# Context rounding moved from ScalarE to GpSimd from the second batch on, with the five engine orders drawn up anew

## The chip, the cores and the metric

The kernel runs on one core of one Trainium2 chip. The metric is the device time of one execution in microseconds (us), the median of several runs. Engines are named as in the profile: PE (TensorE matmuls), PEld (its weight loads), DVE (VectorE), ACT (ScalarE), POOL (GpSimd), SP (SyncE, which issues every DMA here).

## The reference

A gated cross-attention block with a feed-forward network on 16 batches of 224 queries (512 wide) that look at 750 context rows (384 wide):

```python
q = (layernorm(x) @ W_q); k = (context @ W_k); v = (context @ W_v)      # 8 heads of 64
attn = softmax(where(mask, q k^T / 8, -max))
x = x + tanh(g_xattn[0]) * ((attn @ v) @ W_o + b_o)
h = gelu(bitlinear(layernorm(x), w1, b1))
x = x + tanh(g_ffn[0]) * bitlinear(h, w2, b2)
```

`bitlinear` scales each row to 127 levels and the weights to -1, 0 and 1 around the mean of their absolute values, and then multiplies.

## The kernel before

Float32 operands of the attention are split into two float16 tiles, an upper half (the value rounded) and a lower half (the value less its upper half), and every product is three float16 matmuls. The context of a batch is three chunks of 128 x 750 (`KC` = 3). Each chunk is loaded by SP into one of two slots of `ctx_f` (kind LC in the orders); ACT rounds it into `ctx[:, 0, n, :]` (L1199, kind CX), POOL subtracts that from the float32 value into `ctx[:, 1, n, :]` (L1310, also kind CX). `ctx` has one buffer, so the rounding of a batch waits until PE has done all 8 key products (K) and 6 value products (V) of the batch before (`k_proj`, `v_proj`), and the first K or V of a batch waits for `ctx_lo` of all three chunks. The third chunk of a batch takes the slot of the first, so its load waits for the first chunk's subtraction.

PE's other kinds: Q (query products), S (scores), PV (weights times values), O (output projection), F1 and F2 (the two feed-forward products), WM (a product that sums the feed-forward weights' means). The softmax of a batch is 14 units: DVE adds the mask and finds the row extreme (L978, M), ACT takes the exponential (L1157, E) and divides (L1162, N), POOL rounds (L1301, H) and subtracts (L1306, L), and SP turns both halves by a transposing DMA (L740, T) for PV. A slot of `p16` (4) is free again when that DMA has landed.

The feed-forward weights come in 16 float32 pieces: ACT sums absolute values (L1147, WA) into `wabs` and writes a throwaway result into `rough`, which lies over `xc`; after WM, POOL scales each piece (L1290, WB) and DVE clips it (L965, WQ). The first F1 waits for all 16 (`w_quant`). `b1` is loaded (BD) when ten pieces are done.

Nothing is scheduled at run time. Each engine goes through a written list of kind:number:batch (`SP_SEQ`, `PE_SEQ`, `ACT_SEQ`, `DVE_SEQ`, `POOL_SEQ`), and semaphores hold an engine until its operands are there. PE results go through a ring of four PSUM banks, `ps_g0` to `ps_g3`, taken in turn in the order of `PE_SEQ`.

Of the kernel before, what the change touches and what calls it, by code (L numbers as in the profile page):

```python
# [17 lines left out]
HT = TQ // 2  # L18
# [4 lines left out]
NT = 6  # L23
# [4 lines left out]
H = 8  # L28
# [44 lines left out]
def in_order(text):  # L73
# [10 lines left out]
    LC:2:3 XT:1:3 T:1:2 T:0:2 T:3:2 XQ:0:1 T:2:2 LC:1:4 T:4:2 LC:0:4 T:5:2 F2:1:0 LM:0:3 XQ:1:1 T:6:2 LR:1:2 T:7:2
    T:8:2 HT:0:1 T:9:2 LR:0:2 T:11:2 T:12:2 T:10:2 T:13:2 HT:1:1 LC:2:4 T:0:3 LX:0:5 F2:0:1 T:1:3 XT:1:4 XT:0:4
    XQ:0:2 F2:1:1 T:2:3 T:3:3 LR:0:3 T:4:3 T:6:3 LM:0:4 T:5:3 XQ:1:2 T:7:3 T:8:3 T:9:3 LC:0:5 HT:0:2 LR:1:3 T:11:3
    LC:1:5 T:12:3 T:10:3 T:13:3 LC:2:5 LX:0:6 XT:0:5 LM:0:5 XT:1:5 F2:0:2 HT:1:2 T:0:4 XQ:0:3 T:2:4 T:1:4 LR:1:4
    T:3:4 T:4:4 XQ:1:3 F2:1:2 T:5:4 T:6:4 T:7:4 HT:0:3 LC:1:6 T:8:4 LC:0:6 T:9:4 T:10:4 T:11:4 LX:0:7 T:13:4 T:12:4
    XT:0:6 F2:0:3 XT:1:6 HT:1:3 T:0:5 T:1:5 T:2:5 LC:2:6 T:3:5 LM:0:6 T:4:5 T:5:5 LR:0:5 T:6:5 LC:1:7 T:7:5 XQ:1:4
    F2:1:3 T:8:5 LR:1:5 T:9:5 LC:0:7 T:11:5 T:12:5 T:10:5 T:13:5 LM:0:7 LX:0:8 LC:2:7 LR:0:6 XT:0:7 XT:1:7 T:0:6  # L90
    HT:1:4 T:1:6 T:2:6 XQ:0:5 T:3:6 T:4:6 F2:1:4 T:5:6 T:6:6 T:7:6 LC:1:8 LC:0:8 LR:1:6 T:9:6 T:8:6 XQ:1:5 T:10:6
    LM:0:8 HT:0:5 T:11:6 T:12:6 T:13:6 LC:2:8 LX:0:9 XT:1:8 XT:0:8 T:0:7 HT:1:5 T:1:7 T:3:7 T:2:7 XQ:0:6 T:4:7
    F2:1:5 T:5:7 F2:0:5 LR:1:7 LC:0:9 T:7:7 T:6:7 T:9:7 LR:0:7 LC:1:9 XQ:1:6 T:8:7 HT:0:6 T:11:7 T:10:7 T:13:7
# [10 lines left out]
    T:2:13 LM:0:14 T:3:13 T:4:13 F2:1:11 XQ:1:12 T:5:13 LR:1:13 LC:0:15 T:6:13 T:7:13 T:9:13 T:8:13 LM:0:15 T:11:13
    T:10:13 T:12:13 T:13:13 XT:0:15 HT:1:12 LC:2:15 T:0:14 T:1:14 F2:1:12 T:2:14 T:3:14 XQ:0:13 T:5:14 T:4:14
    XT:1:15 T:6:14 LR:0:14 T:7:14 XQ:1:13 HT:0:13 T:8:14 T:9:14 LR:1:14 T:11:14 T:10:14 T:13:14 T:12:14 F2:0:13
    LR:0:15 T:0:15 T:1:15 T:2:15 HT:1:13 T:3:15 XQ:0:14 T:4:15 F2:1:13 T:5:15 T:6:15 T:7:15 T:8:15 LR:1:15 T:9:15
    T:10:15 HT:0:14 T:11:15 T:12:15 T:13:15 F2:1:14 F2:0:14 F2:0:15 F2:1:15
# [351 lines left out]
def build(nc, x_d, ctx_d, mask_d, gx_d, gf_d, wq_d, wk_d, wv_d, wo_d, bo_d, w1_d, b1_d, w2_d, b2_d, out_d):  # L460
    with ExitStack() as stack:
# [937 lines left out]
```

## Time and profile before

| What | Value |
|---|---|
| Median of 3 runs | 1027.44 us (1027.41 to 1028.69) |
| Profiled execution | 1028.62 us, its span 1026.7 us |
| Busy share of the span | PE 95%, ACT 84%, DVE 78%, POOL 76% |
| Costliest line | `ps_g` products of L776, 38% of the chain that ended last |

The span is the part of the execution that the trace covers; the other 1.9 us lie around it. Busy time of matmuls is modelled, so a share of 95% on PE tells that it was seldom without work, not that it ran at its peak. An engine that is idle costs time only where PE, or the end, waits for it.

### The profile page before, as it was taken

How to read it: one execution, taken by the hardware profiler on the slowest of the kernel's cores; microseconds unless marked ns; L12 is line 12 of the kernel's file. 1: busy time of each engine (PE TensorE's matmuls, PEld its weight loads, DVE VectorE, ACT ScalarE, POOL GpSimd, SP SyncE). 2: the span in 40 equal slices, each digit the busy share in tenths (PEclk: the TensorE clock that was granted, in tenths of full speed). 3: DMA queues.
4: the chain of work that ended last, by engine and by line, in shares of the span. 5: the costliest groups of instructions: out<-in, count | busy, mean ns of one | idle time of the engine just before them, and what ended most of it. 6: DMA issues, size and time to landing. Idle time of an engine off the chain costs nothing.

```text
span 1026.7 us, 25406 instructions
## 1 busy us (share of the span) xinstructions
PE 977.3 (95%) x9216; PEld 562.0 (55%) x9216; DVE 800.2 (78%) x1870; ACT 860.0 (84%) x1386; POOL 779.3 (76%) x739
## 2 busy tenths in 40 slices
PE   3979898999999999999999999999999999999887
PEld 2536555565555656555555555555565556556443
DVE  6669788868998677977769778877868776876766
ACT  4879777988879879897888889798897977889866
POOL 3599998787678787877678696877687688867861
PEclk9989999999999999999999999999999999999989
DMA  6999979997879988978879798897888888778961
GB/s 229 239 212 244 206 159 157 177 163 135 189 142 173 187 168 157 169 130 172 155 153 172 157 187 162 137 174 142 169 163 182 166 167 153 138 133 162 168 100 41
DMA packets 472331, 169.10 MB, mean 165 GB/s; under 512 B 450320, under 2 KB 452368, under 8 KB 471824
## 3 DMA queue, kind: packets, MB, share of 16 engines
q1 hardware_dynamic: 472208, 167.48, 83.5%
q8 instruction: 75, 1.23, 0.5%
q14 instruction: 48, 0.39, 0.1%
HBM read 48.28 MB, written 7.34 MB: 54 GB/s over the span
## 4 chain that ended last, share of the span: by engine, by line
PE 68%; DVE 9%; POOL 6%; ACT 6%; DMA 5%; issue 4%; SPq 1%; DVEq 0%; POOLq 0%; ACTq 0%
PE ps_g L776 38%; PE ps_g L826 9%; PE ps_s L809 8%; PE ps_g L864 8%; PE ps_g L901 5%; POOL p L1306 3%; DMA pt<-p 2%; DVE xa L1021 2%; DVE prob L978 1%; POOL ctx L1310 1%; POOL p L1301 1%; ACT prob L1157 1%; ACT prob L1162 1%; DVE xc L1047 1%; ACT h_sb L1255 1%
## 5 line engine op out<-in xcount | busy, mean ns | idle before, releaser
L1306 POOL TENSOR_TENSOR p<-prob,p 128x750 f16<-128x750 f32 x224 | 357.8, 1608 | 4.8
L1301 POOL CAST p<-prob 128x750 f16<-128x750 f32 x224 | 186.0, 835 | 125.7 <-ACT prob L1162 100.1
L978 DVE CUSTOM_DVE_ANT_0 prob<-ps_s,mbias 128x750 f32<-128x750 f32 x224 | 205.8, 933 | 51.3 <-PE ps_s L809 35.2
L1157 ACT ACTIVATE prob<-prob,rmin 128x750 f32<-128x750 f32 x224 | 204.5, 914 | 26.2 <-DVE rmin L978 25.3
L1162 ACT ACTIVATE prob<-prob,rrec 128x750 f32<-128x750 f32 x224 | 198.7, 914 | 29.5 <-DVE rrec L923 29.3
L776 PE MATMUL ps_g<-ctx,wk 128*128 128x375 f16 x1152 | 201.1, 327 | 18.1 <-POOL ctx L1310 17.4
L776 PE MATMUL ps_g<-wv,ctx 128*128 128x512 f16 (+1 forms) x864 | 198.3, 379 | 1.2 <-DVE k_sb L1000 0.6
L776 PEld LDWEIGHTS ps_g<-ctx,wk 128*128 128x128 f16 x1152 | 110.9, 99 | 100.9 <-issue 29.6
L776 PEld LDWEIGHTS ps_g<-wv,ctx 128*128 128x128 f16 (+1 forms) x864 | 86.4, 103 | 97.3 <-issue 6.5
L809 PE MATMUL ps_s<-k_sb,q_sb 64*32 64x375 f16 (+2 forms) x2688 | 129.4, 325 | 7.7 <-DVE k_sb L1000 4.4
L826 PE MATMUL ps_g<-pt,v_sb 128*64 128x224 f16 (+2 forms) x2448 | 121.6, 256 | 4.5 <-DMA pt<-p 4.1
L826 PEld LDWEIGHTS ps_g<-pt,v_sb 128*64 128x64 f16 x2448 | 109.3, 111 | 23.0 <-issue 16.6
L864 PE MATMUL ps_g<-w,xqt 128*128 128x512 fp8e4 x432 | 103.6, 384 | 3.6 <-ACT xqt L1218 2.0
L901 PE MATMUL ps_g<-w,hqt 128*128 128x512 fp8e4 x432 | 97.7, 379 | 3.1 <-DMA hqt<-hq 2.4
L809 PEld LDWEIGHTS ps_s<-k_sb,q_sb 64*32 64x32 f16 (+2 forms) x2688 | 62.4, 95 | 65.5 <-issue 40.2
L1310 POOL TENSOR_TENSOR ctx<-ctx_f,ctx 128x750 f16<-128x750 f32 x47 | 74.1, 1585 | 17.8 <-ACT ctx L1199 17.3
L1075 DVE SCALAR_TENSOR_TENSOR h_sb<-ps_g,sm,b 128x512 f32<-128x512 f32 x108 | 76.8, 744 | 11.3 <-PE ps_g L864 10.7
L994 DVE SCALAR_TENSOR_TENSOR v_sb<-ps_g,v_sb 128x512 f16<-128x512 f32 x96 | 64.9, 685 | 24.3 <-ACT v_sb L1187 23.9
L776 PE MATMUL ps_g<-xt,wq 128*128 128x224 f16 x768 | 82.1, 259 | 0.7 <-DVE wv L931 0.4
L1000 DVE SCALAR_TENSOR_TENSOR k_sb<-ps_g,k_sb 128x375 f16<-128x375 f32 x128 | 67.8, 542 | 18.2 <-ACT k_sb L1174 18.0
L776 PEld LDWEIGHTS ps_g<-xt,wq 128*128 128x128 f16 x768 | 71.9, 98 | 12.9 <-issue 5.3
L776 PE MATMUL ps_g<-wo,attn 128*128 128x512 f16 x336 | 76.7, 380 | 1.3 <-DVE attn L988 1.3
(129 smaller groups left out, 1328.6 us busy)
## 6 DMA issues: line engine op xcount, KB each, us to landing
ctx_f<-in_ctx SPq DMA_DIRECT2D x47, 375.0 KB, 4.0
xa<-in_x SPq DMA_DIRECT2D x16, 448.0 KB, 4.7
xr<-in_x SPq DMA_DIRECT2D x28, 256.0 KB, 3.4
out<-xr SPq DMA_DIRECT2D x28, 256.0 KB, 2.9
pt<-p SPq DMA_TRANSPOSE x254, 4.1
h_sb<-in_w SPq DMA_DIRECT2D x4, 512.0 KB, 5.7
w<-in_w SPq DMA_DIRECT2D x3, 512.0 KB, 6.1
xr<-in_w SPq DMA_DIRECT2D x3, 512.0 KB, 5.0
```

What stands on the lines that cost most here:

```text
L776: mm = nc.tensor.matmul(out, lhs, rhs, start=(m == 0), stop=(m == len(steps) - 1))
L809: mm = nc.tensor.matmul(ps_s[at:at + width, e, c, 0:CH], q_sb[rows, j, qa, q:q + width], k_sb[rows, j, ka, c * CH:(c + 1) * CH], start=(m ...
L826: mm = nc.tensor.matmul(g[e * DH:(e + 1) * DH, 0:size], v_sb[:, p, t, va, (2 * j + e) * DH:(2 * j + e + 1) * DH], pt[:, e, pa * NT + t, pl ...
L864: mm = nc.tensor.matmul(g[:, :], xqt_t[:, k, :], w1v[:, k, f * 512:(f + 1) * 512], start=(k == 0), stop=(k == KD - 1))
L901: mm = nc.tensor.matmul(g[:, :], hqt_t[:, k, :], w2v[:, k, :], start=(k == 0), stop=(k == KF - 1))
L978: nc.vector.tensor_tensor_reduce(prob[:, (b * NU + n) % PROBS, :].rearrange("p (c k) -> p c k", c=2), ps_s[:, n % 2, :, 0:CH], mbias[:, :] ...
L1075: nc.vector.scalar_tensor_tensor(out=h_t[:, f * 512:(f + 1) * 512], in0=g[:, :], scalar=sm2[:, t % 2, 4:5], in1=b1[:, f * 512:(f + 1) * 51 ...
L1157: nc.scalar.activation(prob[:, (b * NU + n) % PROBS, :], prob[:, (b * NU + n) % PROBS, :], ACT.Exp, bias=rmin[:, n:n + 1], scale=-1.0, acc ...
L1162: nc.scalar.activation(held, held, ACT.Copy, scale=rrec[:, n:n + 1]).then_inc(normed, 1)
L1301: nc.gpsimd.tensor_copy(p16[:, u % HILO, 0, 0:J], prob[:, u % PROBS, :]).then_inc(hi_pool, 1)
L1306: nc.gpsimd.tensor_tensor(p16[:, u % HILO, 1, 0:J], prob[:, u % PROBS, :], p16[:, u % HILO, 0, 0:J], ALU.subtract).then_inc(lo_pool, 1)
L1310: nc.gpsimd.tensor_tensor(ctx[:, 1, n, :], ctx_place(b * KC + n), ctx[:, 0, n, :], ALU.subtract)\
```

## The change

ACT keeps the rounding of the context for the first batch only. For batches 1 to 15 POOL does it, just ahead of its own subtraction of the same chunk, with the waits that ACT had. That is 45 instructions. All five lists are drawn up anew. DVE gets two waits at tile 0: the feed-forward's `xc` is written only when all of ACT's sums of absolute values are done (they write into the same place), and the scale is taken only after the second WM.

```diff
@@ lists: 5 of 5 redrawn; the first line of PE_SEQ's second row stands for them @@
-    V:4:0 V:5:0 K:7:0 S:4:0 Q:3:0 WM:0:0 S:5:0 K:0:1 K:1:1 PV:0:0 V:0:1 S:6:0 V:1:1 Q:0:1 K:2:1 K:3:1 Q:1:1 Q:2:1
...
@@ DVE, L2 @@
                     need_tile(dve, "xq", t - 1)
+                    if t == 0:
+                        dve.wait_ge(w_abs, 2 * NW)
                     nc.vector.tensor_scalar(xc[:, :], xr_t, mv2[:, c, 0:1], None, ALU.subtract)\
...
@@ DVE, L3 @@
                     need_tile(dve, "x2_amp", t)
+                    if t == 0:
+                        need(dve, "w_mean", 0, 1)
...
@@ ACT @@
-                elif kind == "CX":
+                elif kind == "CX" and b == 0:
                     need_ctx(act, b * KC + n)
-                    need(act, "k_proj", b - 1, 2 * NP - 1)
-                    need(act, "v_proj", b - 1, NT - 1)
                     nc.scalar.activation(ctx[:, 0, n, :], ctx_place(b * KC + n), ACT.Copy)\
                         .then_inc(s["ctx_hi"], 1)
...
@@ POOL @@
                 elif kind == "CX":
+                    if b > 0:
+                        need_ctx(pool, b * KC + n)
+                        need(pool, "k_proj", b - 1, 2 * NP - 1)
+                        need(pool, "v_proj", b - 1, NT - 1)
+                        nc.gpsimd.tensor_copy(ctx[:, 0, n, :], ctx_place(b * KC + n)).then_inc(s["ctx_hi"], 1)
                     need(pool, "ctx_hi", b, n)
                     nc.gpsimd.tensor_tensor(ctx[:, 1, n, :], ctx_place(b * KC + n), ctx[:, 0, n, :],
```

POOL where the context of batch 1 is made, before (`winv` marks the scaling of weight pieces, `p16` the halves of the softmax):

```order
27 L1301 CAST p16<-prob 128x750
28 L1310 TENSOR_TENSOR ctx<-ctx_f,ctx 128x750
29 L1306 TENSOR_TENSOR p16<-prob,p16 128x750
30 L1290 TENSOR_SCALAR w12<-w12,winv 128x1024
31 L1310 TENSOR_TENSOR ctx<-ctx_f,ctx 128x750
32 L1290 TENSOR_SCALAR w12<-w12,winv 128x1024
33 L1310 TENSOR_TENSOR ctx<-ctx_f,ctx 128x750
```

and after:

```order
30 L1311 CAST ctx<-ctx_f 128x750
31 L1313 TENSOR_TENSOR ctx<-ctx_f,ctx 128x750
32 L1311 CAST ctx<-ctx_f 128x750
33 L1313 TENSOR_TENSOR ctx<-ctx_f,ctx 128x750
34 L1304 TENSOR_TENSOR p16<-prob,p16 128x750
35 L1311 CAST ctx<-ctx_f 128x750
36 L1313 TENSOR_TENSOR ctx<-ctx_f,ctx 128x750
37 L1288 TENSOR_SCALAR w12<-w12,winv 128x1024 x2
```

The two weight pieces that stood between the chunks stand behind them now, and three casts are new.

PE from the last value products of batch 0 to the first key product of batch 1, before:

```order
19 L776 MATMUL ps_g2<-wv,ctx 128x512 x9
20 L776 MATMUL ps_g3<-wv,ctx 110x512 x9
21 L776 MATMUL ps_g0<-ctx,wk 128x375 x9
22 L809 MATMUL ps_s<-k_sb,q_sb 128x375 x12
23 L776 MATMUL ps_g1<-xt,wq 128x224 x12
24 L783 MATMUL ps_g2<-wsum,xqt 128x1
25 L809 MATMUL ps_s<-k_sb,q_sb 32x375 x48
26 L776 MATMUL ps_g3<-ctx,wk 128x375 x9
```

and after:

```order
19 L772 MATMUL ps_g3<-ctx,wk 128x375 x9
20 L772 MATMUL ps_g0<-wv,ctx 110x512 x9
21 L805 MATMUL ps_s<-k_sb,q_sb 64x375 x24
22 L805 MATMUL ps_s<-k_sb,q_sb 128x375 x12
23 L772 MATMUL ps_g1<-xt,wq 128x224 x12
24 L779 MATMUL ps_g2<-wsum,xqt 128x1
25 L805 MATMUL ps_s<-k_sb,q_sb 32x375 x48
26 L772 MATMUL ps_g3<-ctx,wk 128x375 x9
```

One scores unit (64x375, 24 matmuls) moved behind the last value product; the same set of products stands ahead of the first key product of batch 1.

POOL up to the last two weight pieces (those in `h_sb`), before:

```order
73 L1290 TENSOR_SCALAR hq<-hq,winv 128x1024
74 L1306 TENSOR_TENSOR p16<-prob,p16 128x750
75 L1301 CAST p16<-prob 128x750
76 L1290 TENSOR_SCALAR hqt<-hqt,winv 128x1024
77 L1306 TENSOR_TENSOR p16<-prob,p16 128x750
78 L1290 TENSOR_SCALAR xr<-xr,winv 128x1024
79 L1290 TENSOR_SCALAR h_sb<-h_sb,winv 128x1024 x2
```

and after:

```order
79 L1288 TENSOR_SCALAR w12<-w12,winv 128x1024
80 L1288 TENSOR_SCALAR hq<-hq,winv 128x1024
81 L1288 TENSOR_SCALAR hqt<-hqt,winv 128x1024
82 L1299 CAST p16<-prob 128x750
83 L1288 TENSOR_SCALAR xr<-xr,winv 128x1024
84 L1304 TENSOR_TENSOR p16<-prob,p16 128x750
85 L1288 TENSOR_SCALAR h_sb<-h_sb,winv 128x1024 x2
```

The pieces moved a little among the softmax units; counted from the start of the list, everything that stood ahead of the last piece still does, with six context casts (batches 1 and 2) besides.

## Rows read from the trace of the kernel before

**Rows 1.** The page's first part: busy us, share of the span, instructions.

```profile
PE 977.3 (95%) x9216; PEld 562.0 (55%) x9216; DVE 800.2 (78%) x1870; ACT 860.0 (84%) x1386; POOL 779.3 (76%) x739
```

**Rows 2.** Busy time by stretch: start:end, length, engines, granted PE clock, DMA share, GB/s.

```profile
0.00:50.00 50.00, 33.80 (x270) 18.73 (x270) 33.31 (x57) 33.58 (x56) 24.06 (x30) 1.00 0.84 235
50.00:100.00 50.00, 41.89 (x390) 24.37 (x388) 40.41 (x86) 42.17 (x80) 48.18 (x37) 0.90 1.01 219
100.00:150.00 50.00, 46.17 (x500) 28.85 (x496) 40.00 (x93) 37.70 (x68) 46.60 (x42) 1.00 0.93 199
150.00:200.00 50.00, 47.29 (x415) 26.42 (x414) 42.02 (x105) 43.76 (x72) 39.73 (x39) 1.00 0.89 163
...
950.00:1000.00 50.00, 42.44 (x462) 22.55 (x460) 35.72 (x89) 38.35 (x54) 38.65 (x41) 0.90 0.77 136
1000.00:1026.70 26.70, 20.32 (x119) 9.45 (x116) 18.55 (x37) 16.32 (x26) 3.11 (x6) 0.98 0.10 40
```

**Rows 3.** The same view for the middle, 200 to 950 us.

```profile
200.00:950.00 750.00, 745.39 (x7077) 431.63 (x7076) 590.18 (x1410) 648.14 (x1035) 579.00 (x550) 1.00 0.85 161
```

**Rows 4.** PE in order of time, 31 to 66 us: start, us, [idle before <-releaser].

```profile
31.25 3.05 PE L776 MATMUL ps_g<-ctx,wk 128*128 128x375 f16 x18
...
47.64 1.60 PE L776 MATMUL ps_g<-ctx,wk 128*128 128x375 f16 x9
...
53.74 0.38 PE L783 MATMUL ps_g<-wsum,xqt 128*128 128x1 f32 x2 [1.93 <-DVE wsum L958]
58.51 2.08 PE L809 MATMUL ps_s<-k_sb,q_sb 64*32 64x375 f16 x48 [4.39 <-DVE k_sb L1000]
61.74 5.34 PE L776 MATMUL ps_g<-ctx,wk 128*128 128x375 f16 x18 [1.15 <-POOL ctx L1310]
```

**Rows 5.** POOL in order of time, the same place.

```profile
54.99 2.12 POOL L1290 TENSOR_SCALAR w<-w,winv 128x1024 f32<-128x1024 f32 x1 [1.27 <-DVE winv L950]
...
58.57 1.55 POOL L1290 TENSOR_SCALAR w<-w,winv 128x1024 f32<-128x1024 f32 x1
```

**Rows 6.** Groups by line and shape: count, busy us, mean ns, idle before.

```profile
L1301 POOL CAST p<-prob 128x750 f16<-128x750 f32 x224 | 186.0, 835 | 125.7 <-ACT prob L1162 100.1 <-DMA pt<-p 24.5
L1310 POOL TENSOR_TENSOR ctx<-ctx_f,ctx 128x750 f16<-128x750 f32 x47 | 74.1, 1585 | 17.8 <-ACT ctx L1199 17.3
L1199 ACT ACTIVATE ctx<-ctx_f 128x750 f16<-128x750 f32 x47 | 38.2, 823 | 8.1 <-DMA ctx_f<-in_ctx 6.9 <-issue 1.0
```

**Rows 7.** The page's DMA part: issues, KB each, us to landing.

```profile
ctx_f<-in_ctx SPq DMA_DIRECT2D x47, 375.0 KB, 4.0
```

**Rows 8.** POOL, DVE and PE around the last weight pieces, and POOL's wait before them.

```profile
121.45 0.81 POOL L1301 CAST p<-prob 128x750 f16<-128x750 f32 x1 [1.80 <-DMA pt<-p]
...
132.96 2.64 POOL L1290 TENSOR_SCALAR h_sb<-h_sb,winv 128x1024 f32<-128x1024 f32 x2
...
134.99 2.36 DVE L965 TENSOR_SCALAR w<-h_sb 128x1024 fp8e4<-128x1024 f32 x2
...
137.83 3.63 PE L864 MATMUL ps_g<-w,xqt 128*128 128x512 fp8e4 x16
```

**Rows 9.** PE's waits, 130 to 200 us: us in total, times, longest.

```profile
PE ps_g L901 <- DMA hqt<-hq: 1.6, 1, 1.6
PE ps_g L826 <- DMA pt<-p: 0.9, 1, 0.9
```

**Rows 10.** PE in order of time: an output projection, and a second feed-forward product.

```profile
105.58 2.75 PE L776 MATMUL ps_g<-wo,attn 128*128 128x512 f16 x12
...
957.58 3.61 PE L901 MATMUL ps_g<-w,hqt 128*128 128x512 fp8e4 x16
```

**Rows 11.** L1021 alone: shortest, median, longest ns.

```profile
L1021 DVE TENSOR_SCALAR xa<-xa,mv x32: 474/1022/5655, 9.9 to 853.7; 112x512 f32<-112x512 f32 x32
```

**Rows 12.** PE's waits, 950 us to the end, the longest two.

```profile
PE ps_s L809 <- DVE rmin L978: 2.2, 1, 2.2
PE ps_g L864 <- ACT xqt L1218: 2.0, 2, 1.3
```

More of the change, by code:

```diff
@@ L84 @@
[L84 to L93, printed above, removed]
@@ L104 @@
[L104 to L108, printed above, removed]
+    PD:0:0 LX:0:0 LC:0:0 LC:1:0 LC:2:0 PD:1:0 PD:2:0 XT:0:0 XT:1:0 WL:0:0 LM:0:0 WL:1:0 LC:0:1 WL:2:0 LX:0:1 LM:0:1
@@ new lines @@
+    WL:7:0 WL:5:0 WL:6:0 WL:3:0 T:0:0 WL:4:0 T:1:0 LC:1:1 BD:0:0 LC:2:1 PD:3:0 T:2:0 T:4:0 LC:0:2 T:3:0 XT:0:1
+    XT:1:1 T:5:0 LX:0:2 T:6:0 WL:8:0 T:7:0 WL:9:0 LR:1:0 T:9:0 T:8:0 WL:11:0 WL:13:0 WL:10:0 T:10:0 WL:12:0 T:11:0
+    T:13:0 WL:15:0 T:12:0 LC:1:2 WL:14:0 LC:2:2 T:0:1 LM:0:2 T:1:1 XT:0:2 XT:1:2 T:2:1 LC:0:3 T:3:1 LX:0:3 T:5:1
+    T:4:1 T:6:1 T:7:1 XQ:1:0 BD:1:0 LR:1:1 LR:0:1 T:8:1 T:9:1 T:10:1 LM:0:3 T:11:1 LR:0:2 T:12:1 LC:1:3 T:13:1
+    HT:1:0 LX:0:4 XT:0:3 XT:1:3 LC:2:3 T:0:2 T:1:2 XQ:0:1 F2:1:0 T:2:2 T:3:2 T:5:2 T:4:2 T:7:2 XQ:1:1 T:6:2 T:8:2
@@ new lines @@
+    LR:1:8 T:5:8 T:7:8 XQ:1:7 T:9:8 T:8:8 F2:1:6 LC:1:10 HT:0:7 T:11:8 T:10:8 T:13:8 T:12:8 LX:0:11 LM:0:10 T:0:9
+    HT:1:7 LC:2:10 XT:0:10 XT:1:10 T:2:9 T:1:9 T:3:9 F2:0:7 T:4:9 LR:0:9 LR:1:9 XQ:1:8 T:5:9 T:6:9 T:7:9 T:8:9
+    LC:0:11 LM:0:11 T:10:9 T:9:9 LX:0:12 T:11:9 T:13:9 T:12:9 XT:1:11 LC:1:11 XT:0:11 F2:1:7 HT:1:8 T:0:10 LR:0:10
+    LC:2:11 T:1:10 XQ:0:9 T:2:10 T:3:10 LC:0:12 T:4:10 XQ:1:9 T:5:10 F2:1:8 LC:1:12 T:6:10 LX:0:13 T:7:10 T:9:10
+    T:8:10 HT:0:9 T:10:10 T:11:10 T:12:10 T:13:10 LR:1:10 T:0:11 LC:2:12 F2:0:9 T:1:11 XT:1:12 LR:0:11 HT:1:9
@@ new lines @@
+    Q:1:11 N:4:10 L4:0:9 N:5:10 E:8:10 N:6:10 XH:0:12 XH:1:12 N:7:10 E:9:10 N:8:10 L4:1:9 K:0:11 K:1:11 GE:0:9
+    K:2:11 V:0:11 E:10:10 E:11:10 N:9:10 PL:0:10 V:1:11 GS:0:9 V:2:11 N:10:10 E:12:10 V:3:11 N:11:10 K:3:11 G3:0:9
+    K:4:11 E:13:10 E:0:11 N:12:10 PL:1:10 E:1:11 N:13:10 K:5:11 N:0:11 GE:1:9 V:4:11 K:6:11 K:7:11 GS:1:9 E:2:11
+    V:5:11 PL:2:10 N:1:11 PL:3:10 E:3:11 E:4:11 N:2:11 E:5:11 Q:2:11 N:3:11 G3:1:9 Q:3:11 N:4:11 N:5:11 L4:0:10
+    K:0:12 V:0:12 E:6:11 E:7:11 E:8:11 N:6:11 N:7:11 E:9:11 K:1:12 GE:0:10 XH:0:13 V:1:12 E:10:11 V:2:12 Q:0:12
@@ new lines @@
+    N:11:12 E:0:13 N:12:12 N:13:12 K:4:13 E:1:13 K:5:13 PL:1:12 GE:1:11 N:0:13 XH:1:14 K:6:13 N:1:13 GS:1:11 V:4:13
+    E:2:13 K:7:13 E:3:13 G3:1:11 E:4:13 N:2:13 PL:2:12 PL:3:12 V:5:13 E:5:13 Q:3:13 N:3:13 N:4:13 N:5:13 E:6:13
+    E:7:13 V:0:14 K:0:14 N:6:13 L4:1:12 E:8:13 N:7:13 E:9:13 V:1:14 V:2:14 N:8:13 Q:0:14 N:9:13 K:1:14 PL:0:13
+    E:10:13 E:11:13 E:12:13 N:10:13 E:13:13 K:2:14 XH:0:15 K:3:14 N:11:13 XH:1:15 K:4:14 N:12:13 E:0:14 N:13:13
+    E:1:14 V:3:14 Q:1:14 N:0:14 GE:1:12 N:1:14 K:5:14 PL:1:13 E:2:14 E:3:14 Q:2:14 Q:3:14 V:4:14 V:5:14 GS:1:12
@@ new lines @@
+    GM:1:7 VL:4:9 VL:5:9 XH:1:10 QL:2:9 G2:1:7 M:4:9 F2:0:7 PA:2:8 PA:3:8 M:5:9 M:6:9 M:7:9 KL:6:9 N1:0:11 QL:3:9
+    KL:7:9 R:2:9 XN:0:11 R:3:9 O:1:8 L2:1:8 M:8:9 F2:1:7 QL:0:10 M:9:9 QL:1:10 KL:0:10 L3:1:8 XH:0:11 KL:1:10
+    KL:2:10 M:10:9 R:4:9 M:11:9 PA:0:9 F1:4:8 VL:0:10 VL:1:10 R:5:9 M:12:9 M:13:9 F1:5:8 KL:3:10 F1:6:8 R:6:9
+    XH:1:11 F1:7:8 KL:4:10 M:0:10 M:1:10 PA:1:9 M:2:10 VL:2:10 VL:3:10 GM:1:8 R:0:10 VL:4:10 M:3:10 VL:5:10 G2:1:8
+    KL:5:10 KL:6:10 R:1:10 N1:0:12 M:4:10 KL:7:10 QL:2:10 M:5:10 PA:2:9 PA:3:9 XN:0:12 M:6:10 QL:3:10 M:7:10 O:0:9
```

448 lines of the change are left out of this document (217 added, 231 removed).

## The prediction

> **What bounds the kernel now.** I read the page's first part, then the busy time by stretch, then in each stretch where PE idles the order of time and the waits. PE is busy 977.3 of 1026.7 us, ACT 860.0, DVE 800.2, POOL 779.3 [rows 1]. The stretches tell where PE's missing 49.4 us lie: 16.2 in the first 50 us, 8.1, 3.8 and 2.7 in the next three, 7.6 and 6.4 at the end [rows 2], and only 750 - 745.4 = 4.6 us in all the 750 us between [rows 3]. So PE is the bound from 200 to 950 us, and a change that gives PE no less work can win nothing much there; it can lose. What can be won lies between 50 and 200 us (14.6 us of idle time, and in part a lower clock) and after 950 us (14.0 us). The first 16 us are unchanged, since batch 0's context stays with ACT.
>
> Between 50 and 100 us POOL is busy 48.2 of 50 us, from 100 to 150 us 46.6 of 50 [rows 2]. That is the stretch in which POOL scales the feed-forward weights beside the softmax, and it is where the change gives it more.
>
> **What is moved.** ACT loses 45 roundings of 823 ns, 37.0 us. POOL gains 45 casts. The trace has the same cast on POOL, same shape and types, at 835 ns [rows 6]: 45 x 0.835 = 37.6 us, 2.5 us a batch. POOL's share goes from 76% to (779.3 + 37.6) / 1026.7 = 80%, ACT's from 84% to 80%. Neither is the bound by its total. From a chunk's arrival to its lower half the time is the same (0.82 + 1.59 against 0.84 + 1.59), but where ACT rounded the second chunk beside POOL's first subtraction, POOL now does both: the three chunks take 3 x 2.42 = 7.3 us of POOL, against 0.82 + 3 x 1.59 = 5.6 us, 1.7 us more a batch. DVE's two new waits cost nothing: in its own list the sum over all 16 absolute sums and the second WM already stand ahead of them.
>
> **Place 1, the context of batch 1.** Before, PE ends the last key product of batch 0 at 47.64 + 1.60 = 49.2, and starts batch 1 at 61.74, having waited 1.93, 4.39 and 1.15 us between [rows 4]. POOL held it: it idled 1.27 us for the weights' mean, then two weight pieces (2.12 and 1.55 us) stood ahead of the second and third chunk [rows 5]. After, these pieces stand behind. I take the end of batch 0's products at 49.6 (0.4 later, since its last value product now waits for a bank that DVE frees later). POOL then needs 7.3 us and one softmax subtraction of 1.6: 58.5. The third chunk's load starts when the first chunk is done (52.0), takes 0.3 to issue and 4.0 to land [rows 7], so the chunk is done at 56.3 + 2.4 = 58.7. Batch 1 starts at about 58.9, 2.8 us earlier. From both sides: 4 us if the products end at 48.4, 1 us if the load takes as long as 5.8.
>
> **Place 2, the first feed-forward product.** That lead has to survive until F1, which waits for all 16 weight pieces. Before, POOL ended its last piece at 132.96 + 2.64 = 135.6, DVE the clip at 137.3, and PE started F1 at 137.83 [rows 8]; the wait was just covered. POOL is the queue to count here. At about 61.4 it has done the same work in both kernels (the two pieces follow at 58.7, 2.7 us), with three of the new casts already behind it; before, that was at 61.6. From there to the last piece its list holds the same instructions and three more casts, 2.5 us. It had one idle time of 1.80 us there [rows 8] that may be filled. So the last piece ends at 135.6 - 0.2 + 2.5 less 0 to 1.8 = 136.1 to 137.9, I take 137.0. DVE's clip adds 1.7, as before: F1 at 138.7, 0.9 us later than before (0 to 1.8). PE's work ahead of F1 is the same set in both, so here **the whole 2.8 us is given back** and PE waits. This step decides the sum.
>
> **Place 3, 140 to 200 us.** Two waits of PE stand there, 1.6 us for the turned hidden layer and 0.9 us for turned softmax weights [rows 9]. The first hangs on ACT, which has six roundings less behind it, 6 x 0.82 = 4.9 us; it should go. The second hangs on POOL, which is not faster; it stays. I take -1.3, between -2.5 (both go) and +1.5 (POOL late by the third batch's 2.5 us).
>
> **Place 4, the middle.** Thirteen batches from the fourth on. In the new list PE has between 11.4 and 24.5 us of other products after a batch's last key or value product and before the next batch's first, counted with their durations in the trace (an output projection 2.7 and a second feed-forward product 3.5 us [rows 10], some 1.1 us for a scores unit or a query product); POOL has the chunks and what stands between them, 7.3 us and one to four others. The tightest are batch 10 (11.4 us on PE against 7.3 + 1.6 + 0.8 + 0.9 = 10.6 on POOL), batch 15 (12.5 against 10.9) and batch 14 (12.9 against 11.2). Their margins, 0.8 to 1.7 us, hold if POOL comes to them on time. Before, the margins at the same places were 2.3, 1.3 and 4.9. I take +0.7 for the middle, from -1 (ACT's relief takes some of the 4.6 us) to +5.
>
> In the same stretch DVE's L1021 takes 474 ns at best, 1022 in the middle and 5655 at worst [rows 11], in places where POOL works without a pause. The Trainium skill, page "SBUF — State Buffer", section "Who interferes with whom", gives a rule that speaks against the change: a DVE instruction in a two-port mode and a GpSimd instruction take one port pair in turn, and the second fully waits. The trace agrees. By it, DVE's excess at L1021 (32 x (1.022 - 0.474), about 18 us by the median) would grow with POOL's busy time, by 4.8%, some 0.9 us on an engine with 22% idle: the sum would be the same or up to 1 us more.
>
> **Place 5, the end.** The last seven scores and the last tiles keep their order in the main. The two longest waits are 2.2 and 2.0 us [rows 12]. The last scores' row extremes now come ahead of a layer norm on DVE, which takes most of the first; the copy of the turned tile on ACT (the second wait) then stands behind two more normalisations, 1.8 us. I take -0.3, between -2 and +2.
>
> **The sum.** +0.9 (places 1 and 2 together) - 1.3 + 0.7 - 0.3 = 0.0 against the profiled 1028.62 us (span 1026.7). That execution lies at the upper end of the three runs, so against the median of 1027.44 the same sum gives 1027.4 us.
>
> **Rivals.** First, **the lead survives** (faster): POOL reaches its last weight piece early, because it has fewer idle or stretched instructions between 60 and 140 us than I count, and PE's lead of 2.8 us stays, with the waits of place 3. 1027.4 - 0.9 - 2.8 - 1.2 = 1022.5. For it: one place already has POOL idle 1.8 us; against it: POOL has 48.2 of 50 us filled [rows 2]. Chance 0.27. Second, **POOL becomes the gate of each batch's context** (slower): the new 1.7 us per batch falls on PE wherever the margin is used up, which needs POOL to be more than 0.8 to 1.7 us late at its first chunk in the tight batches. Three tight batches only: 3 x 1.7 = +5; half of the thirteen: 6.5 x 1.7 = +11. I take +5, 1032.4. For it: POOL was idle 125.7 us before its casts, waiting for ACT and DMA [rows 6], so it does not run ahead of its work; against it: PE had no wait for the context anywhere in the middle. Chance 0.20. Third, **the clock**: after the idle time at 50 to 60 us 18 key matmuls took 5.34 us at a lower granted clock against 3.05 us at 31 us [rows 4], and the stretch 50 to 100 us has a mean of 0.90 [rows 2]. If the shorter gap keeps the clock up, 2.3 us (and 1 us at the scores ahead) come back, but go into the wait at F1 like the rest; if PE's new wait before F1 (about 3.7 us) brings the clock down, the same 3 us are lost, and stay lost: 1030.5. Chance 0.10. **The change does not do what it says** only if the cast on POOL were dearer than L1301's, at the 1.6 us of a subtraction: 45 x 0.77 = 35 us more of POOL, and the second rival comes true; 0.03, counted there.
>
> **How the numbers follow.** Forecast, within its own range 1025 to 1030: 0.43. The rivals have 0.27 (faster), 0.20 (slower) and 0.10 (slower). A measurement tells apart some 0.2%, 2.05 us. Faster by that: most of the first rival and the lower edge of the forecast, 0.30. Slower: the second, most of the third and the upper edge, 0.31. Within: 0.39. The range takes in the first rival with both waits gone and something won at the end (1021.5), and the second up to four tight batches (1034).
>
> **What would show it.** In the profile of the changed kernel: the first key product of batch 1 at 58 to 60 us; a wait of PE at the first F1 (L860) of 2 to 4 us for DVE's clip, and F1 at 138 to 139.5; L1311 at 0.83 to 0.85 us x45; no longer a wait of 1.6 us for the turned hidden layer; PE busy over 744 us from 200 to 950, with waits for POOL's context absent or under 1 us. It would be wrong if F1 starts before 137, or if PE waits for L1313 in more than three batches, or if the end, from the last key product on, is longer or shorter by over 2 us.

## The result, and the profile of the changed kernel

| | kernel before | changed kernel |
|---|---|---|
| median | 1027.43 us (1027.35 to 1028.69) | 1035.97 us (1035.74 to 1036.46) |
| profiled execution, span | 1026.7 us | 1034.5 us |
| PE idle in the span | 49.4 us | 57.7 us |

The change makes the kernel slower: 1.0072 of before, 95% interval 1.0058 to 1.0087; the medians differ by 8.5 us, the profiled spans by 7.8. The forecast was 1027.4 us, no change, within 1021.5 to 1034, and the time is outside that range. One execution of a later kernel, the one with M:9:12 moved, took 4039 us and is left out of its ratio.

The first part of the page of the changed kernel, against [rows 1]:

```profile
PE 976.8 (94%) x9216; PEld 562.0 (54%) x9216; DVE 801.3 (77%) x1870; ACT 829.0 (80%) x1341; POOL 816.2 (79%) x784
```

PE has the same work. POOL has 36.9 us more. ACT has 31.0 us less: its rounding alone fell from 38.2 to 1.7 us. PE's busy time by stretch (start:end, length, PE, PEld, DVE, ACT, POOL, granted clock, DMA share, GB/s), first of the changed kernel:

```profile
0.00:200.00 200.00, 167.79 (x1552) 97.36 (x1553) 157.81 (x335) 150.50 (x262) 166.17 (x152) 0.99 0.88 200
200.00:780.00 580.00, 575.84 (x5426) 333.94 (x5425) 455.39 (x1099) 481.80 (x773) 474.94 (x458) 1.00 0.87 164
780.00:800.00 20.00, 16.29 (x118) 7.86 (x116) 16.10 (x29) 7.91 (x14) 12.24 (x15) 0.83 0.67 127
800.00:950.00 150.00, 148.08 (x1406) 86.08 (x1405) 112.38 (x267) 125.41 (x201) 114.29 (x107) 1.00 0.82 148
```

and of the kernel before:

```profile
780.00:800.00 20.00, 19.64 (x179) 10.32 (x177) 17.32 (x36) 17.28 (x25) 14.38 (x14) 1.00 0.71 151
```

One stretch of 20 us stands out: PE does 118 matmuls there and not 179, and the granted clock falls to 0.83. To see whether the loss is there, I compared the start of each PE item at which both order lists have issued the same set of items. The changed kernel is 3.2 us ahead at the first key product of batch 1 (61.7 against 58.5), 1.8 behind at the first F1 (137.8, 139.6), even at the first F2 (162.3, 162.4), and from then to O:1:11 (773.7, 774.7) never more than 1.2 us away from it, and 1 us behind at that point. At the next shared point, V:5:13, it is 7.4 us behind (824.8, 832.2), and it ends 7.7 behind. So **about 6.4 us are lost between 775 and 832 us**, and one event near 784 us accounts for them. DVE in order of time there (start, us, then in brackets the idle time before and its releaser):

```profile
783.29 0.68 DVE L1038 BATCH_NORM_STATS2 st<-xr 128x6 f32<-128x512 f32 x1
784.00 0.18 DVE L1040 BATCH_NORM_AGGREGATE mv<-st 128x2 f32<-128x6 f32 x1
784.22 5.56 DVE L1045 TENSOR_SCALAR xc<-xr,mv 128x512 f32<-128x512 f32 x1
789.81 0.69 DVE L1048 TENSOR_REDUCE sm<-xc 128x1 f32<-128x512 f32 x1
790.42 0.93 DVE L974 CUSTOM_DVE_ANT_0 prob<-ps_s,mbias 128x750 f32<-128x750 f32 x1
```

L1045 (L1047 before) takes the mean off the residual row tile in its layer norm, L2:1:11. Its 28 instances take 485 ns at best and 830 in the middle; before, 486, 658, and 1939 at most. This one took 5.56 us. POOL in the same stretch:

```profile
782.46 3.08 POOL L1304 TENSOR_TENSOR p<-prob,p 128x750 f16<-128x750 f32 x2
785.50 2.48 POOL L1350 TENSOR_TENSOR xr<-xr,gb 128x512 f32<-128x512 f32 x2
787.94 1.56 POOL L1299 CAST p<-prob 128x750 f16<-128x750 f32 x2
789.86 1.26 POOL L1350 TENSOR_TENSOR xr<-xr,gb 128x512 f32<-128x512 f32 x1 [0.36 <-DVE xc L1045]
```

POOL's instructions follow each other without a gap until 789.50. There POOL itself stops, since its next entry, L3:1:11, needs this very xc, and 0.28 us later DVE is done. None of these POOL instructions is one of the new casts: two softmax subtractions, two additions of gb2 (the last part of L3:1:10 and L3:0:11) and two softmax casts. PE behind it:

```profile
786.19 1.60 PE L772 MATMUL ps_g<-ctx,wk 128*128 128x375 f16 x9
791.50 2.08 PE L805 MATMUL ps_s<-k_sb,q_sb 64*32 64x375 f16 x48 [3.71 <-DVE rmin L974]
793.51 5.50 PE L860 MATMUL ps_g<-w,xqt 128*128 128x512 fp8e4 x16
```

The scores S:5:12 wait 3.71 us for the minimum that stands behind xc in DVE's list; then 48 score matmuls take 2.08 us (1.15 elsewhere, as in the experiments below) and 16 of F1 5.50 us where 3.63 are usual [rows 8]. From 780 to 790 us the granted clock is 1.00, from 790 to 800 us 0.66: in part of that stretch PE had the lower of its two levels (1.2 for 2.4 GHz), after it had stood idle. The wait and the slower matmuls are 3.7 + 0.9 + 1.9 = 6.5 us, as much as the jump.

### The profile page after: what moved, and what is told of

Read it like the earlier page. It is cut to its first block, busy times and chain, and to the rows that moved or that the text cites. A ratio compares the mean times of both kernels' runs of the same rounds, so it can differ in the third digit from the quotient of the medians.

```text
span 1034.5 us, 25408 instructions
## 1 busy us (share of the span) xinstructions
PE 976.8 (94%) x9216; PEld 562.0 (54%) x9216; DVE 801.3 (77%) x1870; ACT 829.0 (80%) x1341; POOL 816.2 (79%) x784
## 3 DMA queue, kind: packets, MB, share of 16 engines
q8 instruction: 75, 1.23, 0.5%
## 4 chain that ended last, share of the span: by engine, by line
PE 60%; POOL 13%; DVE 10%; issue 7%; ACT 5%; DMA 4%; SPq 1%; POOLq 0%; DVEq 0%; ACTq 0%
PE ps_g L772 33%; PE ps_g L822 7%; PE ps_s L805 7%; PE ps_g L860 6%; PE ps_g L897 5%; POOL p L1304 5%; POOL p L1299 3%; DVE prob L974 2%; DVE xc L1045 2%; DMA pt<-p 2%; POOL ctx L1313 2%; ACT prob L1157 1%; DVE st L1038 1%; DVE xa L1017 1%; SPq L736 1%
## 5 line engine op out<-in xcount | busy, mean ns | idle before, releaser
L1299 POOL CAST p<-prob 128x750 f16<-128x750 f32 x224 | 183.6, 829 | 107.9 <-ACT prob L1162 86.7
L990 DVE SCALAR_TENSOR_TENSOR v_sb<-ps_g,v_sb 128x512 f16<-128x512 f32 x96 | 64.6, 683 | 18.0 <-ACT v_sb L1187 17.8
```

The costliest lines, as they stand in the source:

```text
L1299: nc.gpsimd.tensor_copy(p16[:, u % HILO, 0, 0:J], prob[:, u % PROBS, :]).then_inc(hi_pool, 1)
```

## Experiments

**Theory:** the casts and their order cost nothing together; the loss is DVE's subtraction held off by an unbroken run of POOL work, which the redrawn order happens to make. **Rivals:** the 37 us more of POOL work are the loss; or the redrawn order as a whole is. Times on different chips differ by some 2 us for the same kernel, so I compare ratios to the kernel before run beside each. The expectations give ranges in us; where a time of its own chip would put a run elsewhere in them than its ratio does (the ratio times 1027.4 us), I go by the ratio and say so.

**The move alone.** All five lists are those of the kernel before; POOL's and ACT's code is changed, and DVE has its two new waits at tile 0. In part:

```
-                elif kind == "CX":           (ACT)
+                elif kind == "CX" and b == 0:
+                    if b > 0:                (POOL)
+                        nc.gpsimd.tensor_copy(ctx[:, 0, n, :], ctx_place(b * KC + n)).then_inc(s["ctx_hi"], 1)
```

> The move of the rounding alone: the program of the changed kernel with the five order lists of the kernel before, so that GpSimd makes the 45 casts (0.83 us each) at the places of its own subtractions and ScalarE skips its entries. Theory (the changed kernel loses its 8 us in one event near 784 us, where the subtraction xc<-xr,mv on VectorE took 5.56 us while GpSimd ran without a pause, and that event belongs to the redrawn order): the casts cost next to nothing, 1026 to 1030 us, no xc<-xr,mv over 2.5 us. Rival (the 37 us of added work on GpSimd are the loss): 1032 to 1037 us, with TensorE waiting for the context or for the turned weights in many batches. Second rival (the casts bring the gain of the first 200 us, and the order gives it back): 1022 to 1025 us.

Measured: 1.0133 of before (1.0109 to 1.0157), some 14 us slower, above even what the rival gave; the theory fails here, as it had the casts at next to nothing. The loss is not in one place: against the kernel before it is 4.6 us by the first F2, 6.1 by V:0:4, 8.5 by S:6:8, 10.1 by V:0:13 and 14.1 by V:0:15. One xc took 3.01 us. In PE's waits (total, times, longest), POOL's context has

```profile
PE ps_g L776 <- POOL ctx L1317: 23.5, 7, 16.0
```

where the kernel before has 17.4 us in 3 times; the 16 us at the start are in both. That is 6.1 of the 14 us; the rest is not assigned. What the cast costs apart from held subtractions, the last experiment tells.

**The order alone.** The lists of the changed kernel, rounding by ACT in every batch. ACT's list of the changed kernel has no such entries, so I put them behind the drain or exponential that they followed before, and never ahead of K:7 and V:5 of the last batch; batch 12:

```
-    V:5:11 PL:2:10 N:1:11 PL:3:10 E:3:11 E:4:11 N:2:11 E:5:11 Q:2:11 N:3:11
+    V:5:11 CX:0:12 PL:2:10 N:1:11 PL:3:10 E:3:11 E:4:11 N:2:11 E:5:11 Q:2:11 CX:1:12 CX:2:12 N:3:11
```

> The redrawn order alone: the five order lists of the changed kernel, but the context's upper halves rounded by ScalarE in every batch, its 45 entries put back into ScalarE's list behind the same drain or exponential as in the kernel before; GpSimd keeps only the subtraction. Theory: the run of GpSimd work near 780 to 789.5 us holds no cast, so the event stays, with one xc<-xr,mv of 4 to 6 us and a total of 1033 to 1038 us. Rival (the added work on GpSimd): no cast, no loss, 1026 to 1029 us. Were ScalarE's 33 us at these places now late, waits of TensorE for probabilities would show in many batches, and neither would be borne out.

Measured: 1.0643 (1.0616 to 1.0669), 66 us slower, far outside both. POOL now waits for ACT's rounding in each batch (groups by line; before, this line had 17.8 us of idle time [rows 6]):

```profile
L1312 POOL TENSOR_TENSOR ctx<-ctx_f,ctx 128x750 f16<-128x750 f32 x47 | 74.3, 1585 | 77.6 <-ACT ctx L1201 77.6
```

PE's delay grows at the batch starts, from K:0:1 on. The places of ACT's entries are mine, so this is not the price of the order, only a sign that it can't do with ACT's rounding put in so. But it shows one thing cleanly. With no cast on POOL the event is there again, with the same POOL instructions around it. DVE and then POOL:

```profile
831.20 5.55 DVE L1047 TENSOR_SCALAR xc<-xr,mv 128x512 f32<-128x512 f32 x1
```

```profile
829.43 3.08 POOL L1308 TENSOR_TENSOR p<-prob,p 128x750 f16<-128x750 f32 x2
832.47 2.48 POOL L1349 TENSOR_TENSOR xr<-xr,gb 128x512 f32<-128x512 f32 x2
834.91 1.56 POOL L1303 CAST p<-prob 128x750 f16<-128x750 f32 x2
```

PE waits 4.20 us behind it. The event belongs to the order, not to the casts.

**The run cut short.** Two entries of POOL's list:

```
-    H:4:12 H:5:12 L:4:12 L:5:12 L3:1:10 L3:0:11 H:6:12 H:7:12 L3:1:11 L2:1:11
+    H:4:12 H:5:12 L:4:12 L:5:12 H:6:12 H:7:12 L3:1:11 L2:1:11
```

with L3:1:10 behind L:13:11 and L3:0:11 behind G2:0:11.

> The changed kernel with two entries of GpSimd's list moved, nothing else: the additions of gb2 to the tiles L3:1:10 and L3:0:11, which stand next to each other inside the long run, go to where the kernel before has them (behind L:13:11, and behind G2:0:11). Theory: the run of GpSimd near 784 us is broken, xc<-xr,mv there takes under 2.5 us, TensorE's wait of 3.71 us in front of the scores and the slow matmuls behind it go: 1028 to 1030.5 us. Rival (the loss is spread over the order or the casts and the event only coincides with it): 1034 to 1037 us.

Measured: 1.0044 (1.0029 to 1.0059), 1031.9 us by the ratio, between the two, and the longest xc is 3.12 us and not under 2.5. The expectation was wrong in one point: the run does not end there, since the two casts close up behind the subtractions. It is shorter by 2.48 us, and xc by 2.44. DVE's line alone (ns: shortest, median, longest), PE's wait, and POOL:

```profile
L1045 DVE TENSOR_SCALAR xc<-xr,mv x28: 486/686/3120, 114.2 to 1004.7; 128x512 f32<-128x512 f32 x28
```

```profile
790.65 1.15 PE L805 MATMUL ps_s<-k_sb,q_sb 64*32 64x375 f16 x48 [1.27 <-DVE rmin L974]
```

```profile
784.05 3.09 POOL L1304 TENSOR_TENSOR p<-prob,p 128x750 f16<-128x750 f32 x2
787.08 1.57 POOL L1299 CAST p<-prob 128x750 f16<-128x750 f32 x2
789.01 1.26 POOL L1350 TENSOR_TENSOR xr<-xr,gb 128x512 f32<-128x512 f32 x1 [0.36 <-DVE xc L1045]
```

**The run made longer.** One more sum of constant tiles on POOL behind L3:0:11:

```
+                    nc.gpsimd.tensor_tensor(extra[:, :], gbo[:, :], gb2[:, :], ALU.add)
```

> The changed kernel with one more GpSimd instruction in the long run: a sum of two constant 128x512 tiles into a scratch tile that nothing reads, behind L3:0:11; its output is not used. If VectorE's subtraction is held until GpSimd's run ends, it takes 5.56 plus 1.0 to 1.3 us, 6.5 to 6.9 us, and the kernel 1036.5 to 1039 us. Rival (VectorE gets its turn after a fixed time, or after so many instructions): it stays at 5.6 us or below, and the total at 1035 to 1036.5 us.

The added instruction takes 1.27 us, and xc 6.79, 1.23 more than 5.56. At this place DVE gets no turn after a time or a number of instructions: it waits for POOL's pause. In every trace that has the event (the changed kernel, the order alone, the run cut short, the run made longer, and the one below with M:9:12 moved) xc ends 0.28 us after POOL's pause begins.

```profile
783.54 6.79 DVE L1046 TENSOR_SCALAR xc<-xr,mv 128x512 f32<-128x512 f32 x1
```

```profile
784.82 2.50 POOL L1354 TENSOR_TENSOR xr<-xr,gb 128x512 f32<-128x512 f32 x2
787.26 1.27 POOL L1296 TENSOR_TENSOR extra<-gbo,gb 128x512 f16<-128x512 f32 x1
788.47 1.58 POOL L1303 CAST p<-prob 128x750 f16<-128x750 f32 x2
```

```profile
792.05 2.08 PE L806 MATMUL ps_s<-k_sb,q_sb 64*32 64x375 f16 x48 [4.95 <-DVE rmin L975]
794.07 4.23 PE L861 MATMUL ps_g<-w,xqt 128*128 128x512 fp8e4 x16
```

The total, 1.0076 (1.005 to 1.0102), is the same as that of the changed kernel within the intervals; by the ratio it is 1035.2 us, so the hold came out as the theory had it and the total as the rival had it. PE waited 4.95 us in place of 3.71, but F1 took 4.23 us in place of 5.50 (granted clock 0.83 from 790 to 800 us, 0.66 in the changed kernel). The longer hold cost nothing more, because a shorter part of the work fell to the low clock.

**Another form of the instruction.** The same subtraction, in the form that also sums its output (into an unused column):

```
-                    nc.vector.tensor_scalar(xc[:, :], xr_t, mv2[:, c, 0:1], None, ALU.subtract)\
+                    nc.vector.tensor_scalar(xc[:, :], xr_t, mv2[:, c, 0:1], 0.0, ALU.subtract, ALU.add,
+                                            accum_out=sm2[:, c, 7:8])\
```

 Rival (something else stopped VectorE there, or the order as a whole is slow): an instance of over 4 us stays, or goes without a gain, 1034 to 1037 us.

Measured: 0.9973 of before (0.9958 to 0.9987), 1024.7 us by the ratio and below the theory's range, which is about what the one event alone would give; the changed kernel is now faster than the kernel before. All 28 instances take the same time, though POOL's run stands where it stood (781.22 here, 785.50 there; start, us):

```profile
L1045 DVE TENSOR_SCALAR_CACHE_REDUCE xc<-xr,mv x28: 745/746/747, 112.1 to 996.9; 128x512 f32<-128x512 f32 x28
```

```profile
780.45 0.75 DVE L1045 TENSOR_SCALAR_CACHE_REDUCE xc<-xr,mv 128x512 f32<-128x512 f32 x1
```

```profile
778.18 3.08 POOL L1304 TENSOR_TENSOR p<-prob,p 128x750 f16<-128x750 f32 x2
781.22 2.50 POOL L1350 TENSOR_TENSOR xr<-xr,gb 128x512 f32<-128x512 f32 x2
783.67 1.56 POOL L1299 CAST p<-prob 128x750 f16<-128x750 f32 x2
```

```profile
783.67 1.15 PE L805 MATMUL ps_s<-k_sb,q_sb 64*32 64x375 f16 x48
784.76 3.63 PE L860 MATMUL ps_g<-w,xqt 128*128 128x512 fp8e4 x16
```

The plain form and POOL's run must both be there for the hold. The Trainium skill has this in "SBUF — State Buffer", section "Who interferes with whom": copies and scalar operations of DVE can take a two-port mode and then share a port pair with GpSimd, "not the form that also writes out its accumulator". The trace agrees, 745 to 747 ns in all 28 instances, one of them inside the same POOL run.

The time from S:4:12 to V:5:13, the same PE work in all kernels with the changed PE list, measures the event: 54.8 us in the changed kernel, 50.1 with the run cut, 54.8 with it longer, 48.2 with the summing form (and 48.2 in both runs below that have the summing form for xa too). **The event costs 6.6 us.**

**Who stands behind the held instruction.** One entry of DVE's list:

```
-    L3:0:11 R:3:12 QL:0:13 VL:0:13 L2:1:11 M:9:12 KL:0:13
+    L3:0:11 R:3:12 QL:0:13 VL:0:13 M:9:12 L2:1:11 KL:0:13
```

> The changed kernel with one entry of VectorE's list moved: the mask and minimum M:9:12, for which TensorE's scores wait, stands ahead of L2:1:11, whose subtraction is held. The hold stays (4.3 to 5.6 us, since GpSimd's run is as long as before), but no scores wait behind it. Theory (the price is what queues behind the held instruction on VectorE): TensorE's wait of 3.71 us in front of the scores goes, another of 0 to 2 us for k_sb or for the drains of the first F1 takes its place, total 1030 to 1033 us. Rival (the held tile's own chain sets the loss): 1034.5 to 1036.5 us.

Measured: 1.0029 (1.0014 to 1.0045), by the ratio 1030.4 us, in the theory's range. xc takes 3.74 us, less than the 4.3 to 5.6 expected, since it starts later in the same run, the scores wait for nothing, and a wait of 1.49 us comes up in the middle of F1:

```profile
787.50 3.74 DVE L1044 TENSOR_SCALAR xc<-xr,mv 128x512 f32<-128x512 f32 x1
```

```profile
789.16 1.15 PE L804 MATMUL ps_s<-k_sb,q_sb 64*32 64x375 f16 x48
790.24 1.04 PE L859 MATMUL ps_g<-w,xqt 128*128 128x512 fp8e4 x4
792.77 2.76 PE L859 MATMUL ps_g<-w,xqt 128*128 128x512 fp8e4 x12 [1.49 <-DVE q_sb L1000]
```

The stretch S:4:12 to V:5:13 takes 49.9 us, so this gives back 4.9 of the 6.6 us, some of it through the shorter hold.

**What the change is worth without the hold.** The summing form in the kernel before, first for xc alone, then in either kernel for xc and for xa<-xa,mv (L1021, the same operation on the input rows, [rows 11]).

> The kernel before in its own order, with the same edit as in the one-port run of the changed kernel: xc<-xr,mv in the form that also sums its output (0.745 us in every instance there, where it took 0.658 us in the median and 1.94 at most before). What the held-off subtraction costs the kernel before. Theory: it never was held long there, so little changes, 1026 to 1028.5 us, and the changed kernel with the same edit (0.9973 of before) stays 1 to 3 us faster than this one: that difference is the gain of the change itself with the contention taken out. Rival (the one-port form is a gain of its own in any order): this kernel falls by as much as the changed one against its own former time by more than the one event, to 1023 to 1025 us, and the change itself is worth nothing.

> The changed kernel with both subtractions of VectorE that the two-port form serves (xc<-xr,mv of 28 tiles and xa<-xa,mv of 32 half tiles) in the form that also sums its output. xa<-xa,mv is still held there up to 5.65 us at 10 us, before the first context is ready, and 2.0 to 3.1 us for a pair in five batches. Theory: each pair falls to 1.5 to 1.7 us; at 10 us the held one goes, GpSimd's rs comes earlier or not at all, since TensorE waits for GpSimd's context there and not for xa; total 1023 to 1026.5 us. Rival (all of it was in the one event): the same as the run with xc alone, 1026.4 us, within 0.7 us; or slower by up to 1 us through 32 longer instructions.

> The kernel before, in its own order, with xc<-xr,mv and xa<-xa,mv both in the form that also sums its output: the counterpart of the changed kernel with both (0.9938 of before, interval 0.992 to 0.9957). It says what the change is worth when GpSimd can hold neither subtraction. Theory (with the event gone the change is worth next to nothing, as 0.9973 against 0.9971 with xc alone said): 0.993 to 0.997 of before, 1022.5 to 1025.5 us where before is at 1028, within 2 us of the changed kernel. Rival (the change gains 2 to 4 us that the contention had hidden): 0.9965 to 0.999, over 2.5 us behind the changed kernel of the same form.

> The changed kernel with both subtractions in the summing form, the same program as before, now beside its counterpart on one chip. Theory: 0.992 to 0.996 of before, and within 2 us of the counterpart. Rival: over 2.5 us ahead of it.

Ratios to the kernel before, with their intervals (the two of the middle row come from two chips):

| form of the two subtractions | order and code before | changed kernel |
|---|---|---|
| both plain | 1 | 1.0072 (1.0058 to 1.0087) |
| xc summing | 0.9971 (0.9953 to 0.9989) | 0.9973 (0.9958 to 0.9987) |
| both summing | 0.9933 (0.9911 to 0.9955) | 0.9943 (0.9924 to 0.9962), and 0.9938 (0.992 to 0.9957) on another chip |

Read down, the summing form gains 7 us in the kernel before and 13 in the changed one, though every instance is longer than the plain form at its best (746 against 486 ns; xa 740 against 474). With xc alone the kernel before gains 3 us, where the theory had "little changes": its rival was right, a gain in any order. With both forms its gain is in many small pieces: 1.8 us by the first F2, 4.4 by K:1:6, 7.2 by F1:5:11. The 5.65 us at the start [rows 11] are gone too, and win nothing: at K:0:1 the two are level within 0.5 us. The changed kernel with both gained more than expected, 1021.1 us by the ratio for 1023 to 1026.5. Read across, the change is worth nothing once nothing is held: the differences are within their intervals. The 1 to 3 us that I expected the changed kernel to keep over the other with the same form are not there. All four summing kernels are faster than both kernels of the case; the kernel before with both forms had the lowest median, 1022.21 us beside 1029.6 for the kernel before.

**The move alone, without the hold.**

> The move of the rounding alone (order lists of the kernel before, casts on GpSimd), now with both subtractions in the summing form. With them in the two-port form it took 1.0133 of before, 13 us more. Theory (that loss is the casts standing in an order that was not drawn for them: TensorE waits 6 us more for the context and more through the drains behind it, in many batches, with a single held subtraction of 3.0 us): most stays, 1034 to 1039 us, 6 to 10 us above before. Rival (it too is VectorE held by a busier GpSimd): it goes, 1025 to 1030 us.

Measured: 1.0045 (1.0031 to 1.0058), a median of 1034.3 us. That is 4.7 us above before and not 6 to 10, and 1032.0 us by the ratio, between the two ranges: neither had counted what the summing form gains in any order. So the run to compare with is the kernel before with the same forms (1022.21 us on the same chip), and against it this one is 12 us slower, where the plain forms gave 14. So most of what the casts cost in the old order, 12 us, has nothing to do with held subtractions, and the redrawn order wins these 12 us back, since the changed kernel with both forms is level with the kernel before.

## Why the prediction was wrong, point by point

- **The amount of work moved** was right: L1311 takes 853 ns on average x45 (808 in the middle, 1272 at most), POOL 816.2 us (816.9 forecast).
- **Place 1** was right in its time, K:0:1 at 58.50, forecast 58.9, and 3.2 us earlier than before for 2.8, but in part by luck. Batch 0's products ended at 47.7 us and not at 49.6, so POOL's third chunk was done at 57.3 and not at 58.7; what then stood ahead of K:0:1 was PE's own scores, up to 58.5. PE in order of time, against [rows 4]:

```profile
55.15 0.38 PE L779 MATMUL ps_g<-wsum,xqt 128*128 128x1 f32 x2 [2.00 <-DVE wsum L954]
56.54 2.03 PE L805 MATMUL ps_s<-k_sb,q_sb 64*32 64x375 f16 x48 [1.01 <-DVE q_sb L1001]
58.50 2.36 PE L772 MATMUL ps_g<-ctx,wk 128*128 128x375 f16 x9
```

- **Place 2** was right in what it decides, the lead given back: F1 at 139.59, 1.8 us later than before, at the edge of its bounds (0 to 1.8, +0.9 taken). POOL's last piece (137.6, forecast 137.0) and DVE's clip (138.9, forecast 138.7) ended as counted, and F1 started behind the clip and the drain of v_sb that follows it in DVE's list. But PE did not stand waiting there. At F1 its wait is 0.59 us, not 2 to 4; the lead had gone piece by piece on the way (1.9 us were left at PV:2:0, none at V:2:2), in waits of up to 1.5 us, most of them for DVE, that no term had.

```profile
139.59 3.63 PE L860 MATMUL ps_g<-w,xqt 128*128 128x512 fp8e4 x16 [0.59 <-DVE v_sb L990]
```

- **Place 3**, 140 to 200 us: 1.8 us behind at its start, 1.2 at its end, -0.6 where -1.3 was taken, within its bounds. The wait for the turned hidden layer, 1.6 us before [rows 9], is gone (the longest in the whole run is 0.6 us), and at F2:1:0 the kernel was only 0.1 us behind; 1.1 us of that were lost again by S:6:2 at 191.8 us.
- **Place 4** failed. From 200 to 780 us it held: PE idle 4.2 us for 3.1 before, +1.0 where +0.7 was taken, and no wait for POOL's context in the middle. Then the event adds 6.5 us, and PE's busy time from 200 to 950 us is 740.2, below the 744 given as a sign. The kernel is 1.2 us behind at 208 us and 8.3 at O:0:14 (950.3, 958.6), so the term is +7.1. It is outside the term's upper bound of +5, and it is not the mechanism that this bound was drawn for (POOL late at each batch's context).
- **Where the step failed**: in place 4, the price of the contention. The prediction read 474/1022/5655 ns of L1021, the subtraction on the input rows, took the median, and let the excess grow with POOL's busy share: 0 to +1 us. It never read the same operation in the feed-forward's layer norm, L1047, where the event came. Both lines together took 62.1 us before and 63.0 after, just 0.9 more, but by chance (xa 39.7 and 32.3, xc 22.4 and 30.7), and the total was the wrong measure. One hold of 5.56 us, with the scores' minimum behind it in DVE's list, cost 6.6 us. What counts is how long POOL may go without a pause while DVE has a plain subtraction next, and what waits behind that in DVE's list. The lists show where to look: POOL's entries L:4:12 to H:7:12, none of which waits for L2:1:11, beside L2:1:11 on DVE, with M:9:12 and PE's scores behind it. Whether POOL's entries are all ready by then, the lists alone do not say. I looked for margins of POOL's context only, and never laid POOL's list beside DVE's layer norms. The longest value in the row that I did read, 5655 ns, entered no term, and it is such a hold: in the kernel before DVE's two xa subtractions, the second from 10.27 us, last until 15.92 us, beside POOL's run up to 15.65.

```profile
9.87 6.05 DVE L1021 TENSOR_SCALAR xa<-xa,mv 112x512 f32<-112x512 f32 x2
```

```profile
10.09 0.84 POOL L1326 TENSOR_TENSOR rs<-ve,half_neg 112x2 f32<-112x2 f32 x1
10.90 3.17 POOL L1310 TENSOR_TENSOR ctx<-ctx_f,ctx 128x750 f16<-128x750 f32 x2
14.04 1.61 POOL L1310 TENSOR_TENSOR ctx<-pt,ctx 128x750 f16<-128x750 f32 x1
```

- **The rule of the Trainium skill** that the prediction weighed ("SBUF — State Buffer", "Who interferes with whom") says that the second instruction fully waits for the first. The runs show more: here it waited for the rest of one and then for four (five, in the longer run) that started after it.
- **Place 5**: 8.3 us behind at O:0:14, 7.7 at the end, -0.6 for -0.3, within its bounds. Both parts of it came, the second larger than taken: the wait for the row extreme went from 2.2 us [rows 12] to 0.3, that for ACT's copy of the turned tile from 2.0 to 5.0 (1.8 more was taken).
- **The sum** is then +1.8 - 0.6 + 7.1 - 0.6 = +7.7 us, where +0.9 - 1.3 + 0.7 - 0.3 = 0.0 was forecast. Place 4 is 6.4 of the miss, and the event, at 6.6, is all of that.
- **Rivals.** "The lead survives" did not come about. "POOL becomes the gate" had the right sign and +5 of the 8.5 us (1032.4), but not the mechanism: PE had no wait for the context between 200 and 950 us. The clock did play a part, 2.8 of the 6.5 us, at a wait that no rival had.

## What to carry to other kernels

Before an order is redrawn, lay GpSimd's list beside VectorE's plain copies and scalar operations on SBUF tiles, and look for places where GpSimd has several instructions ready in a row. There VectorE can stand still until GpSimd pauses, and what follows it in VectorE's list waits too. In these traces the rest of GpSimd's run was the most that such an instruction was held, and often it was held for less (see below). Writing such an instruction in a form that needs one port only (here with an accumulator output) costs 0.26 us against its best and took 7 us off this kernel in the old order, 13 in the new; moving the critical instruction ahead of it helps in part. A redistribution between engines and its order are one change: the casts alone lost 12 us in the old order, held subtractions apart, and the new one only won them back.

## What the hardware showed that I had not expected

- A plain 128x512 subtraction on VectorE took 5.56 us, and with one more GpSimd instruction of 1.27 us 6.79 us. It is not always so. Nine of the 28 xc of the changed kernel took over 1.25 us. Two of them were held past the end of a POOL instruction with the next following at once, this one and one of 2.46 us at 712.30; five were let in at the first such boundary, and for two POOL paused there. At 912.86 us of the changed kernel xc took only 1.30 us beside two subtractions on POOL, and POOL's pair was the one that got longer (3.27 us for 3.08): DVE was let in between the two. What decides this at a boundary of POOL's instructions the runs leave open.

```profile
912.26 3.27 POOL L1304 TENSOR_TENSOR p<-prob,p 128x750 f16<-128x750 f32 x2
```

```profile
912.86 1.30 DVE L1045 TENSOR_SCALAR xc<-xr,mv 128x512 f32<-128x512 f32 x1
```

- A longer wait of PE (4.95 for 3.71 us) cost no more in all, as the matmuls after it got the higher clock back sooner.
- The form that takes longer at its best made the kernel faster: 746 ns each time, where the plain one took 486 at best, 658 to 830 in the middle and up to 5557.
